# A two-layer graph network on one core: the norms' halves stored by the first stage, and the order of two loads and of one block of VectorE's work

## What is computed

```python
h = relu(layernorm(x))                            # layer 0
x = x + relu((norm(adj + I) @ h) @ W.T + b)
h = relu(layernorm(x))                            # layer 1; h is "the norms" below
c  = relu(conv17(relu(conv1(h))) + h)             # "the convolution"
s  = h @ w_se.T + b_se
m  = exp(-dist(s, s)) @ relu(h @ w_msg.T + b_msg) # "the messages"
gi = concat(c, m) @ w_ih.T + b_ih
gh = h @ w_hh.T + b_hh
r, z = sigmoid(gi_r + gh_r), sigmoid(gi_z + gh_z)
n = tanh(gi_n + r * gh_n)
x = x + (1 - z) * n + z * h
```

## Time and profile before

| | us |
|---|---|
| median of three runs | 2079.0 |
| lowest and highest | 2076.3 and 2087.9 |
| profiled execution, own time | 2080.8 |
| its span in the profile | 2079.0 |
| PE busy | 1875.2 |
| DVE busy | 1542.4 |
| ACT busy | 1265.4 |
| POOL busy | 1037.1 |

### The profile page before, as it was taken

How to read it: one execution, slowest core, us unless ns; L and a number is a source line. 1 busy time by engine, 2 the same in 40 slices (tenths; PEclk the granted TensorE clock), 3 DMA queues, 4 the chain that set the end, 5 groups by cost and what they waited for, 6 DMA issues and landing times.

```text
span 2079.0 us, 36586 instructions
## 1 busy us (share of the span) xinstructions
PE 1875.2 (90%) x12860; PEld 1772.5 (85%) x12860; DVE 1542.4 (74%) x2737; ACT 1265.4 (61%) x2282; POOL 1037.1 (50%) x1281
## 2 busy tenths in 40 slices
PE   5999999999999999999888988888888888888875
PEld 5999999999999988887788888888788888888875
DVE  8899999998877454446677777777777778777786
ACT  6888888888888664546454544445454554545544
POOL 6788888887666243334533333334333334333441
PEclk9999999999999999999998999999999999989998
DMA  6455556565554456568424343434333343333432
GB/s 197 162 190 192 185 178 208 183 202 177 193 175 138 137 133 151 139 152 204 146 63 90 80 86 81 93 75 86 81 80 89 82 91 88 80 89 72 101 70 46
DMA packets 519058, 263.04 MB, mean 127 GB/s; under 512 B 364903, under 2 KB 493799, under 8 KB 516830
## 3 DMA queue, kind: packets, MB, share of 16 engines
q1 hardware_dynamic: 518878, 260.71, 45.9%
HBM read 151.57 MB, written 109.05 MB: 125 GB/s over the span
## 4 chain that ended last, share of the span: by engine, by line
PE 54%; DVE 25%; ACT 14%; issue 6%; DMA 1%; SPq 0%; POOL 0%; ACTq 0%; DVEq 0%; POOLq 0%
PE P L104 41%; DVE grz L1076 5%; PE P L608 5%; DVE grz L1080 4%; PE P L658 3%; PE P L637 3%; DVE oo L1084 2%; DVE ot L1091 2%; ACT nn L1060 2%; DVE xcf L969 2%; ACT tx0h L937 2%; DVE tf L908 2%; ACT gin L1052 1%; ACT tx2h L937 1%; PE P L629 1%
## 5 line engine op out<-in xcount | busy, mean ns | idle before, releaser
L942 POOL TENSOR_TENSOR tx2l<-tf,tx2h 128x1024 fp32r<-128x1024 f32 x32 | 77.8, 2433 | 261.7 <-ACT tx2h L937 261.7
L104 PE MATMUL P<-tx2h,ws2h 128*128 128x256 f32 x384 | 123.4, 321 | 87.7 <-ACT grz L1027 87.7
L1076 DVE TENSOR_TENSOR grz<-xf,nn 128x512 f32<-128x512 f32 x64 | 111.5, 1742 | 115.5 <-ACT nn L1060 115.5
L104 PE MATMUL P<-tx0h,ws0h 128*128 128x256 f32 x384 | 121.4, 316 | 59.5 <-DVE tx0l L942 59.5
L104 PEld LDWEIGHTS P<-tx2h,ws2h 128*128 128x128 f32 x384 | 83.1, 216 | 92.0 <-ACT grz L1027 92.0
L539 POOL TENSOR_TENSOR axl<-af,axh 128x512 fp32r<-128x512 f32 x64 | 83.5, 1305 | 133.1 <-ACT axh L365 133.1
L977 ACT ACTIVATE xcf<-xcf 128x512 f32<-128x512 f32 x64 | 40.4, 632 | 167.3 <-DVE xcf L969 167.3
L104 PEld LDWEIGHTS P<-tx0h,ws0h 128*128 128x128 f32 x384 | 83.8, 218 | 64.8 <-issue 64.8
L1051 ACT ACTIVATE grz<-grz,cold 128x512 f32<-128x512 f32 x64 | 46.4, 725 | 149.7 <-DVE gin L1036 146.5
L915 ACT CAST bmh<-nf 128x512 fp32r<-128x512 f32 x32 | 19.9, 622 | 170.1 <-DMA nf<-nm_d 168.0
L931 POOL TENSOR_TENSOR last2l<-xf,last2h 128x256 fp32r<-128x256 f32 x32 | 35.8, 1119 | 175.0 <-ACT last2h L926 175.0
(11 more groups left out here) (266 smaller groups left out, 8193.4 us busy)
## 6 DMA issues: line engine op xcount, KB each, us to landing
xh_d<-xst SPq DMA_DIRECT2D x16, 1280.0 KB, 7.6
xl<-xh_d SPq DMA_DIRECT2D x40, 512.0 KB, 6.1
y_d<-yo SPq DMA_DIRECT2D x80, 256.0 KB, 2.4
x<-in_x SPq DMA_DIRECT2D x64, 256.0 KB, 3.0
a<-in_adj SPq DMA_DIRECT2D x64, 256.0 KB, 4.2
at<-in_adjt SPq DMA_DIRECT2D x64, 256.0 KB, 4.5
x_d<-x SPq DMA_DIRECT2D x64, 256.0 KB, 4.8
xn_d<-xt SPq DMA_DIRECT2D x64, 256.0 KB, 4.9
```

Of the source, the lines that this page charges most:

```text
L104: done = e.matmul(o, l, r, start=start, stop=stop, skip_group_check=True)
L942: e.e.tensor_tensor(tx[k][1][:, :, :], tf[k][:, :, :], tx[k][0][:, :, :], ALU.subtract).then_inc(S[LOW[k]], 1)
L1076: e.e.tensor_tensor(wide(rz, 0), xf[p % 3][:, 2 * o:2 * o + 2, :].rearrange("p i t -> p (i t)"), nn[n % 2][:, :], ALU.subtract).then_inc(S ...
```

## The change

- The first stage also stores the halves `xx` of the norms to HBM: all of both halves for even graphs (`xb_d`), the second block of both for odd ones (`xl_d`). The stores are the last entry in SP's list of an iteration, behind the load of taps. They wait for `xxlo`, and the next cast to `xx[0]` waits until they have landed (`sxx`).
- The gates' stage loads the norms' `base` and `last` halves from there (`load_base`, `load_last`) instead of making them on ScalarE and GpSimd.
- In SP's round `load_last` comes first, `load_nm` and `load_base` stand ahead of `load_xn`.
- In `sums_of_blocks` one instruction of two blocks makes the first two differences, and the third sum is made from the second difference.
- In `vector_round` `new_vector` of half-round 1 moves from the end of a round to the next one, behind two `add`s and `sums_low(XC)`.
- Two setup loads share a semaphore.

```diff
@@ -106,13 +106,13 @@
 NAMES = """
-half one ident_in col_in eye2_in w0_in b0_in tt_in w1_in se_in bm_in ft_in gt_in tap0 tap1 s2t
+half one ident_in col_in eye2_in w0_in b0_in tt_in w1_in bm_in ft_in gt_in tap0 tap1 s2t
 consts crs diag rows normrow w1s chi clo ones taps
 ldx0 ldx1 lda0 lda1 lat0 lat1 st0 ag0a ag0 deg0 degm rs0 dd sd sbias hd hdhi hdlo ah ajhi ajlo agg aghi aglo
-out0 u x2 sx20 sx21 st1 ag1a ag1 rs1 n1b xn xnt xt sxt xxhi xxlo s uv cm0 cm1 tcm0 tcm1 h1 mshi mslo
+out0 u x2 sx20 sx21 st1 ag1a ag1 rs1 n1b xn xnt xt sxt sxx xxhi xxlo s uv cm0 cm1 tcm0 tcm1 h1 mshi mslo
 dist af am axhi axlo nmp nm snm dft0 dft1 xe0 xe1 sxh0 sxh1
 unit yz wev0 wev1 lxh0 lxh1 xhi xlo whi wlo wneg wnhi frq ye0 ye1 sy0 sy1 sy2 sy3
-lwt wsum wneg22 whalf wg ly0 ly1 ly2 lxn0 lxn1 lxn2 lnm0 lnm1
+lwt wsum wneg22 whalf wg ly0 ly1 ly2 lxn0 lxn1 lxn2 lxb lnm0 lnm1
 idf xct xcr tx tm tc hix him hic lox lom loc
@@ -134,6 +134,8 @@
     x2_v = x2_d.rearrange(blocked, i=32, q=4, k=32)
+    xb_d = nc.dram_tensor("xb_d", (NP, 2, 128, 2, 256), F32, kind="Internal").ap()
+    xl_d = nc.dram_tensor("xl_d", (NP, 2, 128, 256), F32, kind="Internal").ap()
     y_d = nc.dram_tensor("y_d", (NB, 4 * NT, 256), F32, kind="Internal").ap()
@@ -292,6 +294,16 @@
+            if live(i, 5):
+                b = i - 5
+                e.wait_ge(S["xxlo"], b + 1)
+                for h in range(2):
+                    if b % 2 == 0:
+                        e.e.dma_start(xb_d[b // 2, h], xx[h][:, :].bitcast(F32).rearrange("p (c t) -> p c t", c=2)).then_inc(
+                            S["sxx"], 16)
+                    else:
+                        e.e.dma_start(xl_d[b // 2, h], xx[h][:, 256:512].bitcast(F32)).then_inc(S["sxx"], 16)
+
         def spectrum_out(e, b, c):
@@ -316,6 +328,7 @@
                 e.wait_ge(S["s"], b)
+                e.wait_ge(S["sxx"], 32 * b)
                 e.e.copy(xx[0][:, :], xt[:, :]).then_inc(S["xxhi"], 1)
@@ -861,10 +874,20 @@
             e.wait_ge(S["dl"], 2 * (p - 2))
-            for name in ("tx", "hix", "lox"):
-                e.wait_ge(S[name], 3 * (p - 2))
+            e.wait_ge(S["tx"], 3 * (p - 2))
             e.e.dma_start(xf[p % 3][:, :, :].rearrange("p (c i) t -> p c i t", c=2), xn_d[p]).then_inc(
                 S[f"lxn{p % 3}"], 16)
+
+        def load_base(e, p):
+            e.wait_ge(S["step"], steps(p - 1, 1, IN))
+            for h in range(2):
+                e.e.dma_start(base[XN][h][:, :, :].bitcast(F32), xb_d[p, h]).then_inc(S["lxb"], 16)
+
+        def load_last(e, p):
+            e.wait_ge(S["frq"], 2 * NF)
+            e.wait_ge(S["step"], steps(p - 1, 6, IN))
+            for h in range(2):
+                e.e.dma_start(last[XN][h][:, :].bitcast(F32), xl_d[p, h]).then_inc(S["lxb"], 16)
@@ -897,15 +920,18 @@
+        def sums_done(k, p):
+
+            return p + 1 if k == XN else 3 * p + 2
+
         def sums_of_blocks(e, k, p):
...
             source_in(e, k, p)
-            e.wait_ge(S[HIGH[k]], 3 * p - 1)
-            e.wait_ge(S[LOW[k]], 3 * p - 1)
-            e.e.tensor_tensor(t[:, 1, :], f[:, 1, :], f[:, 0, :], ALU.subtract)
-            e.e.tensor_tensor(t[:, 2, :], f[:, 3, :], f[:, 1, :], ALU.subtract).then_inc(S[SUM[k]], 1)
+            e.wait_ge(S[HIGH[k]], sums_done(k, p - 1))
+            e.wait_ge(S[LOW[k]], sums_done(k, p - 1))
+            e.e.tensor_tensor(t[:, 1:3, :], f[:, 1:4:2, :], f[:, 0:2, :], ALU.subtract).then_inc(S[SUM[k]], 1)
             e.wait_ge(S[SUM[k]], 3 * p + 1)
-            e.e.tensor_tensor(t[:, 0, :], f[:, 3, :], t[:, 1, :], ALU.subtract).then_inc(S[SUM[k]], 1)
+            e.e.tensor_tensor(t[:, 0, :], t[:, 2, :], f[:, 0, :], ALU.add).then_inc(S[SUM[k]], 1)
             e.wait_ge(S[SUM[k]], 3 * p + 2)
@@ -937,7 +963,7 @@
         def sums_low(e, k, p):
-            e.wait_ge(S[HIGH[k]], 3 * p + 2)
+            e.wait_ge(S[HIGH[k]], sums_done(k, p))
             e.wait_ge(S["step"], steps(p - 1, 5, IN))
@@ -979,9 +1005,15 @@
             for k in kinds:
-                n = 3 * p + (1 if j < 2 else 3 if j == 6 else 2)
-                e.wait_ge(S[HIGH[k]], n)
-                e.wait_ge(S[LOW[k]], n)
+                if k == XN and j < 2:
+                    e.wait_ge(S["lxb"], 64 * p + 32)
+                elif k == XN and j == 6:
+
+                    e.wait_ge(S["lxb"], 64 * p + (96 if p + 1 < NP else 64))
+                else:
+                    n = sums_done(k, p) if 2 <= j < 6 else 3 * p + (1 if j < 2 else 3)
+                    e.wait_ge(S[HIGH[k]], n)
+                    e.wait_ge(S[LOW[k]], n)
                 e.wait_ge(S["wg"], 3 - k)
@@ -1103,14 +1135,13 @@
             if now:
-                for k in (XN, NM, XC):
+                for k in (NM, XC):
                     last_high(e, k, p)
...
             if later:
-                base_high(e, XN, p + 1)
                 base_high(e, NM, p + 1)
@@ -1137,6 +1168,7 @@
             if before:
+                new_vector(e, p - 1, 1)
                 gates_vector(e, p - 1, 0)
@@ -1159,15 +1191,12 @@
                 gates_vector(e, p, 1)
-                new_vector(e, p, 1)
...
             if now:
-                last_low(e, XN, p)
                 last_low(e, NM, p)
             if later:
-                base_low(e, XN, p + 1)
                 base_low(e, NM, p + 1)
@@ -1193,6 +1222,7 @@
                 e.wait_ge(S[name], 16 * (NB // 2))
+            e.wait_ge(S["sxx"], 32 * NB)
             for name in ("sxt", "snm"):
@@ -1218,7 +1248,7 @@
             sync.dma_start(st_w1[:, :, :], w1mt.rearrange("(k p) n -> p k n", p=128)).then_inc(S["w1_in"], 16)
-            sync.dma_start(st_se[:, :, :], wset.rearrange("(k p) n -> p k n", p=128)).then_inc(S["se_in"], 16)
+            sync.dma_start(st_se[:, :, :], wset.rearrange("(k p) n -> p k n", p=128)).then_inc(S["w1_in"], 16)
             sync.dma_start(b1m[:, 256:512], bc[:, 1, :]).then_inc(S["bm_in"], 16)
@@ -1241,23 +1271,30 @@
                     load_nm(e, 0)
+                if f == 37:
+                    load_base(e, 0)
                 for chunk in range(2):
...
                 load_y(e, b)
+            load_last(e, 0)
             for p in range(1, 3):
...
             for p in range(NP):
+                if p:
+                    load_last(e, p)
                 for b in (2 * p + 3, 2 * p + 4):
...
                         load_y(e, b)
+                if p and p + 1 < NP:
+                    load_nm(e, p + 1)
+                if p + 1 < NP:
+                    load_base(e, p + 1)
                 if p and p + 2 < NP:
                     load_xn(e, p + 2)
-                if p and p + 1 < NP:
-                    load_nm(e, p + 1)
                 if p:
@@ -1281,7 +1318,7 @@
             scalar.copy(w1m[0][:, :, :], st_w1[:, :, :]).then_inc(S["chi"], 1)
-            e.wait_ge(S["se_in"], 16)
+            e.wait_ge(S["w1_in"], 32)
             scalar.copy(wse[0][:, :, :], st_se[:, :, :]).then_inc(S["chi"], 1)
@@ -1317,8 +1354,6 @@
                     weights_high(e, 2 - (f - 32) // 3)
-                if f == 38:
-                    base_high(e, XN, 0)
             e.wait_ge(S["frq"], 2 * NF)
@@ -1354,7 +1389,7 @@
             e.wait_ge(S["normrow"], 1)
-            e.wait_ge(S["w1_in"], 16)
+            e.wait_ge(S["w1_in"], 32)
             for k in range(2):
@@ -1425,8 +1460,6 @@
             e.wait_ge(S["xlo"], NF)
-            base_low(e, XN, 0)
-            e.wait_ge(S["lox"], 1)
             e.wait_ge(S["wg"], 3)
```

## The result

The changed kernel takes 2129.3 us (median of four runs, 2127.3 to 2131.4) against 2077.6 for the kernel before beside it: a ratio of 1.0245, 95% interval 1.0199 to 1.0291. It is slower by 2.5%. The prediction was slower, 2137 us. The profiled execution has a span of 2129.6 us, against 2079.0 of before.

A forecast was written before the change was run, and what follows sets the result against it. TensorE was taken to bound the first stage, and something making TensorE wait (a chain through VectorE) the gates' stage. 2080.8 + 94 (first-stage loop) - 37 (gates) = 2138 us, given as 2137; range 2045 to 2205, own range 2100 to 2175.

The forecast's parts named there:

- the stores close a loop over SP's wait for taps: First stage: taps' end, store issue, landing, `copy xx` and back to taps take 13.4 us against 10.70; 35 iterations, +94 us.
- The landing: First stage: time for the new stores to land, taken as 3.0 us; 2.0 would give +59, 4.9 +161.
- this wait of 1.44 us: First stage: ScalarE's wait for TensorE between `copy xx` and GpSimd's `axl`, forecast to be gone.
- the sign that the prediction had named: First stage: ScalarE's `copy xx` waits some 4 us for a DMA in 35 iterations of 13 to 13.5 us.
- the order frees TensorE of the wait for `tx0l`: Gates: that wait goes; `gates_vector` starts 1.0 us earlier, at A + 12.6, A being the start of the last block's products.
- The turns in front of `branch_vector`: Gates: GpSimd's earlier messages' work delays L1080 by 1.25, L1084 by 1.15, one L1094 by 0.6: 3.0 us a round.
- TensorE's wait and the clock: Gates: TensorE idles 4.0 us, goes on at A + 27.1, then 27 matmuls take 3.33 to 4.83; round 31.7, -37 us.
- The bound of 33.8 us a round: Gates: slowest case, five us of turns and the slow clock, 33.8 us a round, +29 us.
- the messages' load ahead only costs turns: Gates: loading earlier starts GpSimd's messages' work at about A + 15.3, upon VectorE's second `new_vector`, adding 3.0 us of turns.
- Rival A: Gates win more than the loop costs: no turns, clock up, 28 us a round, -151, total 2024; chance 0.15.
- The halves from HBM: Gates: four ScalarE and GpSimd instructions leave each round, and L1080's 0.97 us of waiting goes.
- SP's queue: Gates: four more DMAs a round join SP's queue, which mostly waits for `new_vector`, so they cost nothing.

The follow-up runs named there:

- e7: Kernel before the change plus only the stores of the norms' halves and the cast's wait for them, in the changed kernel's place: 2205.4 us, ratio 1.0591.
- e1: Changed kernel with the two stores of the norms' halves moved ahead of the load of taps in SP's list: 2021.8 us, ratio 0.9722.
- e6: e1 with the messages' load behind `load_xn` again, as before the change: 1931.9 us, ratio 0.9275.
- e10: e1 with ScalarE's cast of the messages put behind `snap` number 2, loads left as in the change: 1924.2 us, ratio 0.9265.
- e5: Kernel before with VectorE's new order, messages' load ahead and merged subtraction, but the norms' halves made on chip: 2037.4 us, ratio 0.9795.
- e2: Kernel before with only `new_vector` of half-round 1 moved behind the two adds and `sums_low(XC)`: 2027.0 us, ratio 0.9743.
- e4: Kernel before with only the two 256-wide subtractions made one of 512: 2085.3 us, ratio 1.0026.
- e9: e6 with the two stores ahead of the spectra's store as well: 1914.4 us, ratio 0.9218.

## Why the prediction was right, point by point

- **That the stores close a loop over SP's wait for taps** was right. e7 has it alone, e1 takes it away by place alone. The size was low: 2.7 us an iteration and +94 forecast, 3.45 and +121 measured. The landing was about right (3.6 us for the pair of 256 KB stores, 3.0 for the pair of 128 KB, 3.0 taken), the issue of the second store a little quicker (0.76 for 0.95 after the end of taps). The way from the cast to `axl` was 6.43 where I had 6.00: with the wait for TensorE gone, ScalarE waits 0.45 for `ah`. These give 13.6 to 14.3. What is over it, in six iterations of 15.0 to 15.5 us, isn't the landing in five of them (3.5 to 3.8 us), but the way to `axl`, 7.1 to 7.7 us: there the cast had hardly waited for the stores, and ScalarE waits 1.1 to 1.7 us for TensorE at `msh`, as before the change. (In the sixth, both are longer: 6.8 to `axl`, 4.5 to the landing.) The prediction had said that this wait of 1.44 us would be gone; in 16 of the 35 iterations some of it is left. In the mean over the 35 the landing is 3.28 us for 3.0, the way to `axl` 6.62 for 6.00 and the issue of the second store 0.80 for 0.95, and 0.75 us is what the iteration is longer than forecast. Nor were there 35 waits of some 4 us, the sign that the prediction had named, but 31 of 0.3 to 4.6. One such wait at `msh`:

```profile
269.75 0.63 ACT L343 ACTIVATE msh<-tcm 128x512 fp32r<-128x512 f32 x1 [1.66 <-PE P L104]
```

- **That the order frees TensorE of the wait for `tx0l` and brings 1 us, not more**, was right in kind: `gates_vector` starts at A + 12.0, where 12.6 was forecast and 13.6 measured before. The 0.6 less are GpSimd's two `sums_low`, which end at A + 9.6 and not A + 10.1, and the turn of `last_low`, 0.42 us and not 0.7.
- **The turns in front of `branch_vector`**: 1.25, 1.15 and 0.6 forecast, 3.0 together; 0.98, 0.95 and 0.49 measured, 2.4. The earlier trace rows had shown 0.97 us of delay for just such a GpSimd instruction, and I should have taken it as it stood.
- **TensorE's wait and the clock**: 27.1 us forecast, 25.8 measured, then 4.83 us for 27 matmuls, the slow row that I had leaned to. A round of 31.7 against 30.63, so -37 against -72. This term was mis-sized by half, mostly by the two points above; both errors were 1.1 to 0.8 us a round or iteration, and they went opposite ways in the sum: +27 and -35. That is why 2137 is near 2129. The path and the signs were right, but that the total is within 8 us is luck: the single terms were further off than it. (The bound of 33.8 us a round, for five us of turns and the slow clock, is a slip: its terms 12.6 + 10.3 + 5 + 1.19 + 4.83 give 33.9, so +32 and not +29.)
- **That the messages' load ahead only costs turns**: right, and stronger than I wrote it. I counted its 3.0 us of turns as a part of the change's round and weighed it with the rest. e6 and e10 measure what hangs on it, in the kernel with the rest of the change: 3.0 and 3.2 us a round, 90 to 98 us, more than the gates' stage won in all. Of that 1.8 to 1.9 us are TensorE's wait, and 1.1 to 1.4 the clock behind it. Rival A had both, no turns and full clock, and was priced at 28 us a round; when its condition was met the round was 27.4 to 27.6.
- **The halves from HBM** were taken as 0.97 us a round (L1080's wait), which with the messages early is what e5 and e1 show (1.0). With the messages late they are worth more than that, 31.19 in e2 against 27.56 in e6, where merging is in the difference too (by itself it won nothing, e4). I had not seen that the two hang together.
- **SP's queue**: that four DMAs more a round cost nothing is as forecast as far as can be seen: TensorE waits for none of these loads in the gates' stage of the changed kernel, e1, e6 or e9. No run leaves out the DMAs alone. That the spectra's store would hold the new stores in every fourth iteration, once the loop is gone, I had not seen; it is hidden while the loop is there.

## What to carry to other kernels

A store added to the end of a DMA queue's list inherits every wait ahead of it; if something on the compute side then waits for its landing, look for the loop that this closes, and put the store ahead of the long wait and of large transfers. Where two engines take turns at SBUF, a late load can be what keeps them apart: before making it early, ask what it will start, and beside which instructions of the chain; the start can also be held back on the engine that makes the work ready. Measure such parts one by one and in pairs: here two moves that each brought the round to 27.2 us gave 28.2 together, a load that ScalarE had awaited in nearly every round cost 37 us when it alone was made early, and two large effects of opposite sign had nearly hidden each other.

## What was not expected of the hardware

That a waiting instruction gets in at the other engine's next boundary, and how far this stretches both. L1108 takes 2.90 us beside GpSimd's 3.40, the additions that read PSUM (L1068) keep 0.68 beside GpSimd's first, and VectorE's `sums_low` slips in between GpSimd's two, which makes the second 3.40 us where it had been 2.42. The Trainium skill, SBUF — State Buffer (Who interferes with whom), says that a VectorE instruction with two SBUF inputs contends with a GpSimd instruction that reads SBUF, and that one with at most one SBUF input doesn't, outside its two-port modes; the traces agree.

In the iterations shown a pair of stores landed 3.6 us (256 KB each) and 3.0 us (128 KB each) after the issue of the second, and 7.9 us after it behind 1280 KB of spectra. By the formula of the Trainium skill, DMA: Bandwidth & Descriptors (Anatomy of one DMA), which is a fit for DMAs issued by GpSimd, the estimate for one DMA of 256 KB was 2.6 us; the 3.6 and 7.9 us measured are above it.
